# First layer: two banks of their own for the turned weights in the attention; in the row phase, ScalarE normalises and the stages stand one pair further apart

## What is computed

```python
x = x + _L0_conv_ref(_gn(x), ...)          # _gn: group norm, 32 groups of 4 channels
xn = (x - mu) * rsqrt(var + EPS) * ln_w + ln_b              # over the channels, at each position
tri_bias = einsum('bijd,dh->bhij', xn, w_tri)[:, None]      # 4 heads
mask_bias = INF * (mask[:, :, None, None, :] - 1.0)
q, k, v = xn @ w_q / sqrt(C), xn @ w_k, xn @ w_v            # 4 heads of 32
scores = einsum('bimhc,binhc->bihmn', q, k) + tri_bias + mask_bias
o = einsum('bihmn,binhc->bimhc', softmax(scores), v)        # attention within each of the 256 rows
o = sigmoid(xn @ w_g + b_g) * o
return o @ w_o + b_o
```

## Time and profile before

| | |
|---|---|
| runs | 27172.97 us median of 3 (27160.68 to 27182.06) |
| the profiled execution | 27187.59 us; its span 27185.8 us, mean PE clock 0.958 |
| busy in the whole span | DVE 93%, ACT 87%, POOL 86%, PE 80% |
| row phase | about 112 to 692 us |
| attention | about 705 to 2908 us |
| layer 1 | the rest, from about 2.9 ms |

### The profile page before, as it was taken

One profiled execution on the slowest core, in us unless ns is written; L12 is line 12 of the kernel. 1 busy time (PEld: TensorE's weight loads), 2 busy tenths in 40 slices (PEclk: granted clock), 3 DMA queues, 4 the chain that ended last, 5 costly groups with the idle time before them and its releaser, 6 DMA issues.

```text
span 27185.8 us, 494791 instructions
## 1 busy us (share of the span) xinstructions
PE 21719.7 (80%) x145198; PEld 16495.5 (61%) x145198; DVE 25255.5 (93%) x23743; ACT 23580.4 (87%) x48522; POOL 23338.1 (86%) x10372
## 2 busy tenths in 40 slices
PE   5888588888888888888888888888888888888887
PEld 1666366666666666666666666666666666666666
DVE  7777599999999999999999999999999999999999
ACT  2677499999999999999999999999999999999998
POOL 4000299999999999999999999999999999999999
PEclk6999799999999999999999999999999999999999
DMA  4111433333333333333333333333333333333333
GB/s 149 49 47 47 147 109 108 108 108 110 107 111 108 108 109 107 109 108 109 108 109 106 110 108 109 109 107 110 109 108 108 108 108 108 107 108 109 108 109 97
DMA packets 2189148, 2868.62 MB, mean 106 GB/s; under 512 B 695002, under 2 KB 964858, under 8 KB 2177786
## 3 DMA queue, kind: packets, MB, share of 16 engines
q1 hardware_dynamic: 2181978, 2803.33, 33.7%
q10 hardware_dynamic: 4608, 33.82, 0.3%
HBM read 2667.01 MB, written 169.74 MB: 104 GB/s over the span
## 4 chain that ended last, share of the span: by engine, by line
ACT 34%; PE 23%; issue 17%; DVE 11%; POOL 3%; ACTq 1%; DVEq 0%; POOLq 0%
DVE hst L1535 9%; ACT dbT L1424 8%; ACT dAs L1402 8%; PE yps L1240 7%; ACT dA L1402 6%; PE misc L1141 5%; PE dbx L1225 5%; ACT vab L1357 2%; PE misc L1177 2%; PE misc L1160 2%; POOL hc L1612 2%; DVE hc L1543 1%; ACT dbx L1402 1%; ACT vab L1343 1%; POOL dbu L1598 1%
## 5 line engine op out<-in xcount | busy, mean ns | idle before, releaser
L1598 POOL TENSOR_TENSOR dbu<-dtu,bb 128x1024 f32<-128x1024 f32 x4096 | 9699.4, 2375 | 867.0 <-DVE hst L1535 859.8
L1535 DVE TENSOR_TENSOR_SCAN hst<-dA,dbu 128x1024 f32<-128x1024 f32 x4096 | 9348.4, 2282 | 494.9 <-ACT dA L1402 417.8
L1612 POOL TENSOR_TENSOR hc<-hst,cc 128x1024 f32<-128x1024 f32 x4096 | 9734.0, 2376 | 4.9 <-DVE hst L1535 4.5
L1240 PE MATMUL yps<-ident,hc 128*128 128x128 f32 x65536 | 8781.6, 280 | 348.2 <-POOL hc L1612 343.5
L1240 PEld LDWEIGHTS yps<-ident,hc 128*128 128x128 f32 x65536 | 7809.8, 145 | 1479.9 <-issue 797.3
L1535 DVE TENSOR_TENSOR_SCAN hst<-dAs,dbx 128x1024 f32<-128x1024 f32 x3584 | 8118.4, 2265 | 102.2 <-ACT dAs L1402 51.7
L1225 PE MATMUL dbx<-ident,dbT 128*128 128x128 f32 x28672 | 4061.3, 287 | 3024.4 <-DVE hst L1535 2713.6
L1424 ACT ACTIVATE dbT<-dtuT,bT 128x256 f32<-128x256 f32 x14336 | 6124.6, 495 | 18.2
L1225 PEld LDWEIGHTS dbx<-ident,dbT 128*128 128x128 f32 x28672 | 3309.8, 146 | 4385.5 <-DVE hst L1535 3366.5
L1402 ACT ACTIVATE dA<-dtv,aneg 128x508 f32<-128x508 f32 x8192 | 5289.2, 678 | 371.6 <-DVE hst L1535 365.8
L1402 ACT ACTIVATE dAs<-dtv,aneg 128x508 f32<-128x508 f32 x7168 | 4741.1, 710 | 385.1 <-DVE hst L1535 385.0
(11 more groups left out here) (187 smaller groups left out, 25487.1 us busy)
## 6 DMA issues: line engine op xcount, KB each, us to landing
bb<-l_bscr SPq DMA_DIRECT2D x1024, 1024.0 KB, 5.7
cc<-l_bscr SPq DMA_DIRECT2D x1024, 1024.0 KB, 5.5
bx<-l_bscr SPq DMA_DIRECT2D x1024, 256.0 KB, 6.1
xg<-xgp SPq DMA_DIRECT2D x512, 85.0 KB, 2.3
xgp<-xb ACTq DMA_DIRECT2D x32, 1032.0 KB, 9.4
xt<-in_x_dram SPq DMA_DIRECT2D x128, 256.0 KB, 2.8
l_xnT<-xo SPq DMA_DIRECT2D x128, 256.0 KB, 2.0
xn<-l_xnT SPq DMA_DIRECT2D x256, 128.0 KB, 2.1
```

What stands on the lines that cost most here:

```text
L1240: mm = pe.matmul(yps[:, p, f * P:(f + 1) * P], hc[:, u % HB, f * 512 + p * P:f * 512 + (p + 1) * P], ident[:], is_transpose=True, start=fi ...
L1535: nc.vector.tensor_tensor_scan(hst[:, v % 4, way], decays.rearrange("p f c -> p (f c)")[:, way], inputs.rearrange("p f c -> p (f c)")[:, way],
L1598: nc.gpsimd.tensor_tensor(to, dtu[:, step % 2], row.unsqueeze(1).to_broadcast([P, 2, 512]), ALU.mult).then_inc(s_inp, 1)
L1612: nc.gpsimd.tensor_tensor(hc[:, v % HB].rearrange("p (f c) -> p f c", f=2), hst[:, v % 4].rearrange("p (f c) -> p f c", f=2), row.unsqueez ...
```

## The change

*Row phase.* There is a fourth stage, "fin" (t-3). DVE no longer applies the normalisation; it makes nb = -mean x rstd (one scalar_tensor_tensor on 128 x 4) in "mid", and in "fin" takes over the negated copy of the bias out of PSUM. ACT applies xh x rstd + nb in "mid", four Identity activations of 128 columns with scale and bias from SBUF. Its evacuation of the transposes, PE's bias matmul and SP's store of xnT move from one stage to the next ("end"), SP's store of the bias to "fin". PE does the transposes of t-1 first, then the bias matmul of t-2.

*Attention.* The turned weights leave the scores' banks: heads 0 and 2 go to bank 6 (copied out by DVE), heads 1 and 3 to bank 7 (copied by ACT, one more than before). The weighted sums share bank 0 with q and k, the output shares bank 1 with v and gate, the factors share bank 6. The projections are made a turn ahead, q and k apart from v and gate, and all three engines have a new order. x is added to the output by a transpose in place of a matmul. SP loads xn two rows ahead.

```diff
-                        if "mid" in stages:
-                            store_xn(t - 1, (h - 1) % BUFS)
                         if "end" in stages:
-                            store_bias(t - 2, (h - 2) % BUFS)
+                            store_xn(t - 2, (h - 2) % BUFS)
+                        if "fin" in stages:
+                            store_bias(t - 3, (h - 3) % BUFS)
...
                         if "mid" in stages:
-                            dve.wait_ge(s_rc, t)
-                            for a in range(W2):
-                                last = nc.vector.tensor_scalar(xh[:, m, a], xh[:, m, a], mv0[:, m, a, 0:1], sd[:, m, a:a + 1],
-                                                               ALU.subtract, ALU.mult)
-                            last.then_inc(s_ln, 1)
+                            dve.wait_ge(s_rc, t * 2 - 1)
+                            nc.vector.scalar_tensor_tensor(out=nb[:, m], in0=mv0[:, m, :, 0], scalar=-1.0, in1=sd[:, m],
+                                                           op0=ALU.mult, op1=ALU.mult).then_inc(s_rc, 1)
+                        if "fin" in stages:
+                            e = (h - 3) % BUFS
+                            dve.wait_ge(s_b, t - 2)
+                            wait(dve, s_st[e], dmas(t - 3, e))
+                            nc.vector.tensor_scalar(tr[:, e], pb[:, (h - 3) % 2], -1.0, None, ALU.mult).then_inc(s_tr, 1)
...
+                        if "mid" in stages:
+                            m = (h - 1) % BUFS
+                            act.wait_ge(s_rc, t * 2)
+                            for a in range(W2):
+                                last = nc.scalar.activation(xh[:, m, a], xh[:, m, a], ACT.Identity, bias=nb[:, m, a:a + 1], scale=sd[:, m, a:a + 1])
+                            last.then_inc(s_ln, 1)
...
-            ps_qk, ps_vg, ps_o, ps_x = (banks[:, b] for b in (0, 1, 6, 7))
+            ps_qk, ps_vg = banks[:, 0], banks[:, 1]
+            ps_out, ps_o = banks[:, 1, 0:N], banks[:, 0, 0:N]
+            ps_f = banks[:, 6, 0:N]
...
-                        wait(pe, s_tv, r * 3)
-                        wait(pe, s_ta, r)
+                        wait(pe, s_sm, r * NH)
...
+                    def turned(r, h, d):
+
+                        pe.wait_ge(s_ex, r * NH + (d + 1))
+                        if d == 0:
+                            wait(pe, s_fc, r)
+                        elif d == 2:
+                            pe.wait_ge(s_tv, r * 2 + 1)
+                        else:
+                            wait(pe, s_ta, r * 2 + d // 2)
...
-                            mm = pe.matmul(dst, xr[:, h, a], ident0[:], start=False, stop=True)
...
+                            mm = pe.matmul(dst, xr[:, h, a], ident0[:], is_transpose=True, start=False, stop=True, skip_group_check=True)
...
                         if "new" in stages:
                             scores(r, h)
                         if "mid" in stages:
+                            turned(r - 1, 1 - h, 0)
+                            turned(r - 1, 1 - h, 1)
+                        if "next" in stages:
+                            project_qk(r + 1, 1 - h)
+                        if "mid" in stages:
+                            turned(r - 1, 1 - h, 2)
+                            turned(r - 1, 1 - h, 3)
+                        if "end" in stages:
+                            output(r - 2, h)
+                        if "next" in stages:
+                            pe.wait_ge(s_qe, r + 2)
+                        if "mid" in stages:
                             sums(r - 1, 1 - h)
                             turn_factors(r - 1)
+                        if "next" in stages:
+                            project_vg(r + 1, 1 - h)
...
+                        def turn_out(d):
+                            act.wait_ge(s_tf, r * NH + (d + 1 - NH))
+                            wait(act, s_o, r - 1)
+                            nc.scalar.copy(pT[:, d].rearrange("p k n -> p (k n)"), banks[:, 7]).then_inc(s_ta, 1)
                         if "new" in stages:
-                            act.wait_ge(s_qk, r + 1)
-                            wait(act, s_sc, r * NH - NH)
-                            nc.scalar.mul(qk[:, h, 0], ps_qk[:, 0:N], float(-1.0 / HD ** 0.5))
-                            nc.scalar.copy(qk[:, h, 1], ps_qk[:, N:2 * N]).then_inc(s_qe, 1)
+                            act.wait_ge(s_ve, r * 2 + 2)
+                            nc.scalar.activation(ge[:, h], ge[:, h], ACT.Tanh, scale=0.5).then_inc(s_ge, 1)
                         if "mid" in stages:
-                            act.wait_ge(s_tf, r * NH + (2 - NH))
-                            wait(act, s_o, r - 1)
-                            nc.scalar.copy(pT[:, 1].rearrange("p k n -> p (k n)"), banks[:, 3]).then_inc(s_ta, 1)
+                            turn_out(1)
+                        if "new" in stages:
+                            weights(0)
+                        if "next" in stages:
+                            copy_qk(r + 1, 1 - h)
+                        if "mid" in stages:
+                            turn_out(3)
+                        if "new" in stages:
+                            weights(1)
                         if "end" in stages:
                             act.wait_ge(s_xf, r - 1)
                             wait(act, s_out[h], turns(r - 2, h))
                             wait(act, s_bn, r - 3)
-                            nc.scalar.activation(xo1[:, h], ps_x[:, N:2 * N], ACT.Identity, bias=bo[:]).then_inc(s_xe, 1)
+                            nc.scalar.activation(xo1[:, h], ps_out, ACT.Identity, bias=bo[:]).then_inc(s_xe, 1)
                         if "new" in stages:
-                            act.wait_ge(s_ve, r * 2 + 2)
-                            nc.scalar.activation(ge[:, h], ge[:, h], ACT.Tanh, scale=0.5).then_inc(s_ge, 1)
-                        for d in range(NH):
-                            if "mid" in stages and d == 1:
-                                act.wait_ge(s_gt, r)
-                                wait(act, s_gs, r - 1)
-                                nc.scalar.mul(fT[:], ps_x[:, 0:N], 0.5).then_inc(s_fc, 1)
-                            if "new" in stages:
-                                act.wait_ge(s_sm, r * NH + (d + 1))
-                                for a in range(NT):
-                                    last = nc.scalar.activation(ss[:, h, d, a], ss[:, h, d, a], ACT.Exp, scale=-1.0, bias=nmx[:, h, d, a:a + 1],
-                                                                accum_out=se[:, h, a, d:d + 1])
-                                last.then_inc(s_ex, 1)
+                            weights(2)
+                        if "mid" in stages:
+                            act.wait_ge(s_gt, r)
...
-                                nc.vector.tensor_copy(pT[:, d].rearrange("p k n -> p (k n)"), banks[:, 2 + d]).then_inc(s_tv, 1)
+                        def top(d):
+                            dve.wait_ge(s_sc, r * NH + (d + 1))
+                            nc.vector.memset(held1[:, NH * h + d:NH * h + d + 1], 0.0)
+                            for a in range(NT):
+                                last = nc.vector.tensor_tensor_reduce(ss[:, h, d, a], banks[:, 2 + d, a * N:(a + 1) * N], tri[:, a, d],
+                                                                      1.0, 3.0e38, ALU.add, ALU.min, nmx[:, h, d, a:a + 1])
+                            last.then_inc(s_sm, 1)
+
+                        def turn_out(d):
+                            dve.wait_ge(s_tf, r * NH + (d + 1 - NH))
+                            wait(dve, s_o, r - 1)
+                            nc.vector.tensor_copy(pT[:, d].rearrange("p k n -> p (k n)"), banks[:, 6]).then_inc(s_tv, 1)
                         if "new" in stages:
                             dve.wait_ge(s_vg, r + 1)
                             vg = ps_vg.rearrange("p (a k c) -> p a k c", a=NT, k=2)
                             nc.vector.tensor_copy(vv[:, h], vg[:, :, 0]).then_inc(s_ve, 1)
                             nc.vector.tensor_tensor(ge[:, h], vg[:, :, 1], bg[:].unsqueeze(1).to_broadcast([P, NT, P]), ALU.add).then_inc(s_ve, 1)
+                            top(0)
                         if "mid" in stages:
+                            turn_out(0)
                             factors(r - 1, 1 - h)
                         if "new" in stages:
-                            for d in range(NH):
-                                dve.wait_ge(s_sc, r * NH + (d + 1))
-                                nc.vector.memset(held1[:, NH * h + d:NH * h + d + 1], 0.0)
-                                for a in range(NT):
-                                    last = nc.vector.tensor_tensor_reduce(ss[:, h, d, a], banks[:, 2 + d, a * N:(a + 1) * N], tri[:, a, d],
-                                                                          1.0, 3.0e38, ALU.add, ALU.min, nmx[:, h, d, a:a + 1])
-                                last.then_inc(s_sm, 1)
```

(37 more changed lines are left out.)

104 lines of the change are left out of this document (55 added, 49 removed).

## The result

The changed kernel took 27017.17 us (median of 4 runs, 27007.19 to 27020.66) beside 27175.75 of the kernel before (4 runs, 27160.68 to 27182.06): a ratio of 0.9941, interval [0.993, 0.9953], faster by 0.6%. The forecast was 26,770 with a range of 26,640 to 26,960: the sign was right, the gain was 159 us instead of 406, and the time lies outside the range.

What follows compares the result with a forecast made beforehand. Attention bound by a ring through ACT, PE and DVE, row phase by the chain from POOL through the store to the next load: 323 + 82 less some 3 gives 402 us, so 26,770 us, range 26,640 to 26,960.

Steps and rivals of the forecast that it cites:

- it keeps its code, so I cost it at nothing: Layer 1, behind both changed stages: no change in its time, within 21 us either way.
- 323 us forecast: Attention: gain from 8.59 to 7.33 us a row over 256 rows.
- the forecast's second ring: Attention: ACT through the factors' copy, DVE's product, v and g, tanh, to head 1's copy; 7.13 us a row.
- the forecast's own ring: Attention: ACT's exponentials, copies and output evacuation, PE's v and g, scores, transposes, head 1's copy; 7.24 us, taken as binding.
- the 0.09 for the loop's jump: Attention: added to the ring's 7.24 us, giving 7.33 us a row.
- handoffs dearer: Rival, 22%: near-equal rings rarely mesh; attention 7.9 us a row, row phase 3.9 a pair, 26,933 us in all.
- 82 us forecast: Row phase: gain from 4.39 to 3.75 us a pair over 128 pairs.
- the 3.57 of the chain: Row phase: us a pair if DVE's product never waits; POOL, ACT, SP and load make 10.71 us for three pairs.
- the 3.9 with the port: Row phase: us a pair if DVE's product waits for POOL's hold of the SBUF port; gain then 63 us.
- the 3.75 chosen: Row phase: us a pair, taken between 3.57 without a port wait and 3.9 with it.
- PE's clock didn't fall: Rival "slower", 3%: TensorE's clock falls from 1.00 in attention; 28,450 us if all rows fall to the lower level.
- 95%: Attention: PE's busy share reaching this was a sign of the forecast being wrong; rival "PE becomes the bound" had 13%.

Runs made afterwards that it cites:

- p_fix: Changed kernel plus idle always-met waits ahead of layer 1, shifting each engine's code by a multiple of 256 instructions against the kernel before; 26852.82 us.
- r_both: p_fix with ACT's output evacuation ahead of head 1's exponentials and the factors' transposes behind v and gate; 26829.13 us, timed again 26841.69, 0.9876 of the kernel before.
- r_mm: Changed kernel, without idle waits, with the residual x added by a matmul again instead of a transpose; 27772.11 us, attention 7.549 us a row.

## Why the prediction was wrong

**Layer 1, "it keeps its code, so I cost it at nothing".** This step failed and took the time out of the range: 187 us where up to 21 was allowed. The prediction's own sign of being wrong, a layer 1 longer by more than 20 us, is what came. The text stayed, its place didn't, and p_fix shows the size by putting it back: 26,853, inside the range. The sentence even named "a changed place of its instructions", but priced it with the spread of runs of one and the same binary, which can't contain it. No row of before showed the price; the rows that pointed at it were 917.4 us of PEld's waits on "issue" and ten 16 KB packets a batch, in a stage of 24 ms. With such a stage behind the change, one microsecond a batch is 128 us.

**Attention: 323 us forecast, 1.05 x 256 = 269 measured.** The mechanism was right in the main: the scores' wait of 0.94 us is gone, and three queues mesh in a ring. But the ring is another one. What PE still waits for stands before the sums (0.37 us, for ACT's copy of head 3) and not before v and gate; ACT's wait before the copy of head 1 (0.29) stands where said. Three steps were wrong. (1) The binding ring is the one through the copy of head 3 and the sums, which the prediction didn't add up: of the sums it listed only the wait "for the copy of q and k", which stands just ahead of head 3's copy on ACT. (2) v and gate to the scores took 1.03, not 0.87, where the scores follow them: "PEld banks L452 <- issue", a wait of the scores' weight load, totals 44.1 us in 133 rows, 0.33 each. In r_both, where the factors follow v and gate, the step is 0.96. That the weight load is the reason is likely, not tested; the step adds 0.16 to each ring that runs through it. (3) The exponentials of two heads take 2.00, not 1.96. The evacuation's 0.38 from start to start, in the forecast's second ring, stands in no row of before; it measures 0.35 (1506.11 to 1506.46). By the measured terms the forecast's own ring is 7.47 and the one through the sums 7.55; the 0.09 for the loop's jump isn't seen on top. The forecast's second ring of 7.13 measures 7.16 (4.81 on ACT from 1502.64 to the factors' copy at 1507.45, 0.47 to the product, 1.01 to the gate, 0.45 to the tanh, 0.42 to the copy of head 1). The rival "handoffs dearer" had 7.9; 7.545 lies between it and the forecast, and for another reason.

**Row phase: 82 us forecast, 93 measured** (0.726 x 128), with no loss from one more turn of filling. 3.66 lies between the 3.57 of the chain and the 3.9 with the port. That it came so near the 3.75 chosen is in part luck: between the bounds nothing priced how often the product would meet POOL. The chain's 0.20 for the square root stands in no row either (its row lasts 0.30); in the changed kernel the Identities start 0.21 behind it. The port wait is there, in some pairs:

```profile
L259 DVE SCALAR_TENSOR_TENSOR nb<-mv,sd x128: 127/144/1199, 124.1 to 587.7; 128x4 f32<-128x4 f32 x128
...
  ACT xh L278: 19.9, 39
```

The product of 128 x 4 took 0.14 us in the middle and up to 1.20; ACT's Identities waited for it 39 times, 19.9 us in all. A timeline shows one of them meeting POOL's operation:

```profile
409.12 1.26 POOL L220 TENSOR_TENSOR xh<-xt,gmx 128x512 f32<-128x512 f32 x1 [1.14 <-DMA xt<-in_x_dram]
409.22 1.18 DVE L259 SCALAR_TENSOR_TENSOR nb<-mv,sd 128x4 f32<-128x4 f32 x1
...
410.44 1.65 ACT L278 ACTIVATE xh<-xh,nb,sd 128x128 f32<-128x128 f32 x4 [0.80 <-DVE nb L259]
```

By the rule of the Trainium skill in SBUF — State Buffer, Who interferes with whom, the small instruction waits for the port's whole hold; this row agrees, but the product mostly slips in ahead of POOL, so that 3.9 wasn't reached. Four Identities take 1.63 to 1.65 us, 0.48 each at a pitch of 0.39; the forecast was 1.52 and 0.48, 0.38. POOL still ends its idle time with the load of x, as said:

```profile
POOL xh L220 <- DMA xt<-in_x_dram: 246.2, 106, 116.4
```

Without the first load's 116.4 that is 129.8 us in 105 waits; before, 334.9 - 115.6 = 219.3 in 116.

**The rivals.** PE's clock didn't fall: 1.00 over the attention with more transposes than before (20 a row for 18), which goes against the rule that the prediction took from the Trainium skill, TensorE: Matmul & The Clock Gate, Part 4: PE-mode transpose. PE's busy share did reach 95%, which the prediction had as a sign of PE being the bound; r_mm shows that the sign was badly chosen, since a busy row counts time inside a ring too. No rival had layer 1 in it.

**The sum.** 402 forecast, 357.5 seen at the first scan, -187.1 behind it. Of the 44 us that are missing ahead of layer 1 the attention lacks 54 and the row phase gives 11 more.

## What to carry to other kernels

When a change alters the number of instructions ahead of a long loop that is loaded anew in each pass, look at whether the loop's own time has moved: here it moved by up to 939 us of 24 ms, more than twice what the change gained ahead of it. Read the loop's first and last start before and after, and look for "<- issue" waits and instruction packets in it; if they changed, pad the code ahead as in p_fix, so that each engine's shift is a multiple of 256 instructions, before judging the change. And when a wait is taken out of a ring, add up every ring through the new queues, and price a step by what stands next to it in the new order, as v and gate show (0.87 before, 1.03 with the scores behind them).

## What the hardware showed unexpectedly

- 296 instructions of always-met waits on PE ahead of layer 1 cost 151 us in the loop behind them, 256 cost nothing (-36), and 40 PE instructions on top of the change's cost 752 more (24,104 to 24,856). Each of these kernels ran once.
- 99 instructions on ACT alone cost 107 us without a single "PE ... <- issue" wait; DVE's wait for PE's L1204 grew to 234.2 us from 174.1. How ACT's place reaches the end is not settled.
- The row phase's mean granted clock rose from 0.57 to 0.81 with PE's busy time falling from 360.94 to 320.32 us. PE is no bound there, and no run tested why.
